# A block of gated delta rule and experts on one core: 8x8 diagonal blocks inverted on GpSimd, the order of the pieces laid out over four turns, and a pipelined first stage

## What is computed

```
q, k = l2norm(silu(conv4(h @ Wq))), l2norm(silu(conv4(h @ Wk)));  v = silu(conv4(h @ Wv))
g = -exp(A_log) * softplus(h @ Wa + dt_bias);  beta = sigmoid(h @ Wb)
for each token:  S = S * exp(g);  delta = (v - k S) * beta;  S = S + k^T delta;  o = (q * scale) S
o = rmsnorm(o, gnorm_w) * silu(h @ Wg);  out = h2 + (silu(ff @ W1) * (ff @ W3)) @ W2,  h2 = h + o @ Wo
```

## Time and profile before

| | |
|---|---|
| median of 3 runs | 2630.22 us (2629.96 to 2634.56) |
| profiled execution, its own time | 2633.98 us |
| its span | 2632.2 us |
| PE, PEld busy | 2466.6 (94%), 2063.6 us (78%) |
| DVE, ACT, POOL busy | 2057.6 (78%), 1689.0 (64%), 899.0 us (34%) |
| mean granted clock of TensorE | 0.967 |

### The profile page before, as it was taken

One profiled execution on the slowest core, in us unless ns is written; L12 is line 12 of the kernel. 1 busy time (PEld: TensorE's weight loads), 2 busy tenths in 40 slices (PEclk: granted clock), 3 DMA queues, 4 the chain that ended last, 5 costly groups with the idle time before them and its releaser, 6 DMA issues. The chain is left out here.

```text
span 2632.2 us, 59594 instructions
## 1 busy us (share of the span) xinstructions
PE 2466.6 (94%) x21984; PEld 2063.6 (78%) x21984; DVE 2057.6 (78%) x4303; ACT 1689.0 (64%) x3890; POOL 899.0 (34%) x1053
## 2 busy tenths in 40 slices
PE   1289999999999999999999999999999999789997
PEld 0168888888888888888888888888888888646655
DVE  3468888888888888888888888888888888535444
ACT  1157777777777777777777777777777777522221
POOL 0033444444444444444444444444444444100000
PEclk6589999999999999999999999999999999889998
DMA  2221121112111211121112111121112110031000
GB/s 98 86 57 40 41 60 42 41 41 60 42 41 42 60 41 41 42 60 41 42 41 56 45 42 41 52 49 42 41 45 56 41 42 14 1 121 32 33 6 11
DMA packets 148317, 120.45 MB, mean 46 GB/s; under 512 B 24305, under 2 KB 128698, under 8 KB 148034
## 3 DMA queue, kind: packets, MB, share of 16 engines
q1 hardware_dynamic: 148034, 116.66, 16.7%
HBM read 72.11 MB, written 2.54 MB: 28 GB/s over the span
## 5 line engine op out<-in xcount | busy, mean ns | idle before, releaser
L740 DVE TENSOR_TENSOR dr_w<-dr_ps,mask 128x512 bf16<-128x512 f32 x768 | 526.3, 685 | 90.5 <-PE dr_ps L556 89.7
L754 DVE SCALAR_TENSOR_TENSOR dr_y<-dr_ps,dr_cw,dr_y 128x255 f32<-128x255 f32 (+2 forms) x1152 | 475.8, 474 | 38.1 <-ACT dr_y L870 38.1
L856 ACT CAST dr_tn<-dr_ps 128x512 bf16<-128x512 f32 x640 | 375.0, 586 | 157.6 <-PE dr_ps L569 156.7
L859 ACT CAST dr_tt<-dr_ps 128x512 bf16<-128x512 f32 x768 | 459.2, 598 | 20.9 <-PE dr_ps L576 20.9
L653 PE MATMUL dr_ps<-dr_w,dr_am 128*128 128x96 f32 x3072 | 418.2, 279 | 9.5 <-ACT dr_w L916 2.1
L653 PEld LDWEIGHTS dr_ps<-dr_w,dr_am 128*128 128x128 f32 x3072 | 378.8, 193 | 32.3 <-ACT dr_w L916 24.5
L870 ACT ACTIVATE dr_y<-dr_ps,dr_cw 128x256 f32<-128x256 f32 x384 | 160.9, 470 | 222.2 <-PE dr_ps L593 222.1
L576 PE MATMUL dr_ps<-dr_tt,dr_w 128*128 128x128 bf16 x3072 | 297.6, 219 | 0.9 <-DVE dr_w L740 0.9
L556 PE MATMUL dr_ps<-dr_tn,dr_b 128*128 128x128 bf16 x3072 | 297.6, 219 | 0.0
L982 POOL TENSOR_SCALAR_AFFINE_SELECT dr_b<-dr_b 128x512 bf16<-128x512 bf16 x128 | 81.6, 637 | 506.9 <-ACT dr_b L906 506.9
L569 PEld LDWEIGHTS dr_ps<-dr_w,dr_tt 128*128 128x128 bf16 x2560 | 186.7, 101 | 84.5 <-issue 49.3
(11 more groups left out here) (188 smaller groups left out, 4784.2 us busy)
## 6 DMA issues: line engine op xcount, KB each, us to landing
dr_abc<-scr_a SPq DMA_DIRECT2D x64, 512.0 KB, 5.6
dr_qk<-dr_sy SPq DMA_DIRECT2D x384, 48.0 KB, 2.0
dr_hb<-hT SPq DMA_DIRECT2D x64, 256.0 KB, 2.5
dr_bcb<-scr_b SPq DMA_DIRECT2D x128, 64.0 KB, 4.7
dr_qk<-dr_sy SPq DMA_DIRECT2D x128, 32.0 KB, 1.9
ex_modb<-scr_mod SPq DMA_DIRECT2D x4, 1024.0 KB, 8.2
dr_wo<-in_Wo SPq DMA_DIRECT2D x1, 3072.0 KB, 10.9
dr_wv<-in_Wv SPq DMA_DIRECT2D x8, 384.0 KB, 4.0
```

Of the source, the lines that this page charges most:

```text
L740: v.tensor_tensor((tn if l == 0 else w16)[:, us, :], ps[:, (X0, X1)[g], :].rearrange("p (u n) -> p u n", u=QH), bc(mask[:, l, :], 1, QH), ...
L754: v.scalar_tensor_tensor(y[:, slot, x:T], ps[:, BANK[n], off:off + T - x], cw[:, t, TAPS - 1 - x:TAPS - x], y[:, slot, x:T], ALU.mult, ALU ...
L856: act.copy(tn[:, us, :], ps[:, (X2, X1)[g], :].rearrange("p (u n) -> p u n", u=QH)).then_inc(s["tn_ok"], 1)
L859: act.copy(dst, ps[:, (X0, X2)[g], :].rearrange("p (u n) -> p u n", u=QH)).then_inc(s["tt_ok"], 1)
```

## The change

**The inverse.** LEVELS goes from 7 to 4: the levels of sizes 1, 2 and 4 go, and the diagonal blocks of size BASE = 8 come from elsewhere. SP moves the diagonal 16x16 pieces of b16 to c16 (eight transfers for each iteration, piece `blocks`). PE spreads the rows of each block over its partitions with 14 products against a selection matrix (`rows`), ACT copies them to ab. POOL then solves all 8x8 blocks by substitution, in a copy and 14 instructions, each waiting for the one ahead (`base`). DVE widens the result to blocks of 32 in c32, transposes it, and writes tt and tn of 128x128 with two multiplies of 1024 elements (`expand`). Level 0 is now a full level with both products of merge2.

**The order.** PLAN is new: places up to 57.07, stage and slot as before (15 slots, depth 4, now over 64 + 3 turns too). values is later by a turn, base and expand stand at the end of the second turn, the merges in the third. The gate pieces come after decayed, in banks A0 and A1, and free them for proj of the next turn. hb is gone; PE reads hT itself. SP loads the gate weights apart from the others, after batch. The semaphores that counted passed waits are gone.

**The first stage.** All groups are written out and interleaved over the engines; the modulation's first 512 columns come first, are spread over the partitions by PE and not by way of DRAM; the remaining 1024 columns follow later. ACT centres, POOL takes half of the scaling, the step matmuls follow each group. Weights of the next stage (wqk, wv, cw, wo, gw) are loaded here.

```diff
-LEVELS = 7
+BASE = 8
+LEVELS = 4
+LVL0 = 3
...
+PLAN = ((0.41, ("proj", 0)), (1.58, ("taps", 0, 0)), (1.83, ("taps", 0, 1)), (1.87, ("proj", 1)),
+        (3.4, ("taps", 1, 0)), (4.13, ("silu", 0)), (5.57, ("taps", 1, 1)), (7.06, ("silu", 1)), (7.19, ("proj", 2)),
+        (8.17, ("taps", 2, 0)), (9.44, ("taps", 2, 1)), (9.53, ("gains",)), (10.1, ("norms",)), (10.15, ("keys",)),
+        (10.23, ("decays", 0)), (10.86, ("keys_scale",)), (11.0, ("decayed", 0, 0)), (11.07, ("decayed", 0, 1)),
+        (11.47, ("scores", 0)), (11.59, ("silu", 2)), (12.87, ("decays", 1)), (13.09, ("scores", 1)),
+        (13.39, ("decayed", 1, 0)), (13.6, ("decayed", 1, 1)), (13.76, ("negate", 0)), (13.94, ("gate", 0)),
+        (14.49, ("negate", 1)), (14.94, ("gate", 1)), (20.05, ("values", 0)), (21.7, ("values", 1)),
+        (25.51, ("rows",)), (27.18, ("base",)), (28.56, ("round", 0)), (29.84, ("expand",)),
+        (31.0, ("merge1", 0, 0)), (31.19, ("merge2", 0, 0)), (31.2, ("merge1", 0, 1)), (31.72, ("merge2", 0, 1)),
+        (31.77, ("merge1", 1, 0)), (32.28, ("merge2", 1, 0)), (32.77, ("merge1", 1, 1)), (34.03, ("merge2", 1, 1)),
+        (35.01, ("merge1", 2, 0)), (35.76, ("merge2", 2, 0)), (36.28, ("merge1", 2, 1)), (37.74, ("merge2", 2, 1)),
+        (38.13, ("merge1", 3, 0)), (38.59, ("merge2", 3, 0)), (38.74, ("merge1", 3, 1)), (38.82, ("merge2", 3, 1)),
+        (39.8, ("w0", 0)), (40.13, ("residual", 0, 0)), (40.72, ("delta", 0, 0)), (41.66, ("residual", 0, 1)),
+        (42.95, ("delta", 0, 1)), (43.63, ("state_out",)), (43.75, ("mean", 0)), (44.13, ("ks",)),
+        (45.27, ("w0", 1)), (45.87, ("gated", 0)), (46.18, ("residual", 1, 0)), (46.5, ("oT", 0)),
+        (46.7, ("delta", 1, 0)), (48.42, ("residual", 1, 1)), (50.02, ("wo", 0)), (50.69, ("delta", 1, 1)),
+        (52.48, ("acc", 0)), (53.27, ("out", 1)), (53.95, ("mean", 1)), (55.15, ("gated", 1)), (56.28, ("oT", 1)),
+        (56.8, ("wo", 1)), (57.07, ("acc", 1)))
...
+            def spread(b):
+                wait(pe, s["bc_free"], b - NBC + 1)
+                pe.matmul(ps[:, BC + b % NBC, :], bc(const[0:B, C_ID + b], 1, P), mod[:, 0:2 * D],
+                          start=True, stop=True).then_inc(s["bc_ps"], 1)
...
+            def blocks(it):
+                m = it % NB
+                sp.wait_ge(s["b16_ok"], (it + 1) * CH)
+                wait(sp, s["bc_ps"], it)
+                for n in range(P // (2 * BASE)):
+                    rows = slice(2 * BASE * n, 2 * BASE * (n + 1))
+                    sp.dma_start(c16[rows], b16[rows, m, :, rows]).then_inc(s["c_st"], 16)
...
+            def rows_(st):
+                it, m = st
+                pe.wait_ge(s["c_st"], (it + 1) * 16 * (P // (2 * BASE)))
+                wait(pe, s["tt_ok"], it * LEVELS * 2 - 1)
+                for j in range(BASE - 1):
+                    for h in range(2):
+                        last = pe.matmul(ps[:, X0, j * U * BASE:(j + 1) * U * BASE], sel[:, h, j, :],
+                                         c16[:, :, h * BASE:(h + 1) * BASE], start=(h == 0), stop=(h == 1))
+                last.then_inc(s["bc_ps"], 1)
...
-                pe.wait_ge(*((s["tap"], (it + 1) * NT * 3), (s["gs_ok"], it * CH + 1))[c])
+                if c == 0:
+                    pe.wait_ge(s["wg_ld"], (it // B + 1) * 16)
+                pe.wait_ge(s["am_ok"], it * 4 + 3 + c)
...
+            def expand(st):
+                it, m = st
+                v.wait_ge(s["xb_ok"], it + 1)
+                v.tensor_tensor(c32[:].rearrange("p u (r i) -> p u r i", r=4), bc(xb[:], 2, 4),
+                                bc(bc(const[:, C_QUART:C_QUART + 4], 1, U), 3, BASE), ALU.mult).then_inc(s["c32_ok"], 1)
+                v.wait_ge(s["c32_ok"], it + 1)
+                v.transpose(c32t[:].rearrange("p u i -> p (u i)"), c32[:].rearrange("p u i -> p (u i)")
+                            ).then_inc(s["c32t_ok"], 1)
+                wait(v, s["p3"], it * LEVELS * 2)
+                blk = bc(bd32[:].rearrange("p (n i) -> p n i", i=4 * BASE), 1, U)
+                v.tensor_tensor(tt[:].rearrange("p u (n i) -> p u n i", i=4 * BASE), bc(c32[:], 2, 4), blk,
+                                ALU.mult).then_inc(s["te_ok"], 1)
+                v.wait_ge(s["c32t_ok"], it + 1)
+                v.tensor_tensor(tn[:].rearrange("p u (n i) -> p u n i", i=4 * BASE), bc(c32t[:], 2, 4), blk,
+                                ALU.mult).then_inc(s["te_ok"], 1)
...
+            def base(st):
+                it, m = st
+                n = it * (2 * BASE - 2)
+                wait(pool, s["c32_ok"], it)
+                pool.tensor_copy(xb[:], bc(const[:, C_UNIT:C_UNIT + BASE], 1, U)).then_inc(s["xs"], 1)
+                pool.wait_ge(s["ab_ok"], it + 1)
+                for j in range(BASE - 1):
+                    left = BASE - 1 - j
+                    pool.wait_ge(s["xs"], n + 2 * j + 1)
+                    pool.tensor_tensor(xt[:, :, 0:left], bc(xb[:, :, j], 2, left), ab[:, j, :, j + 1:BASE],
+                                       ALU.mult).then_inc(s["xs"], 1)
+                    pool.wait_ge(s["xs"], n + 2 * j + 2)
+                    ins = pool.tensor_tensor(xb[:, :, j + 1:BASE], xb[:, :, j + 1:BASE], xt[:, :, 0:left], ALU.add)
+                    ins.then_inc(s["xb_ok"] if j == BASE - 2 else s["xs"], 1)
```

More of the change, by code:

```diff
@@ L58 @@
 ATANH = [1.0 / (2 * k + 1) for k in range(9)]
[L60 to L66, removed]
[7 rows of a table removed]
[L74 to L79, removed]
@@ L89, in wait @@
         eng.wait_ge(sem, value)
[L92 to L106, removed]
 class Chain:
@@ L242, in _, with steps @@
-            pe.wait_ge(beta_ok, 1)
+                        last = pe.transpose(ps[:, TR + k, j * P:(j + 1) * P], hn[:, g % 2, j, k * P:(k + 1) * P],
+                                            const[:, C_ID:C_ID + P])
+                    last.then_inc(s["tr_ps"], 1)
+            def steps(g):
+                pe.wait_ge(s["ht_ok"], (g + 1) * KT)
+                for w in range(2):
+                    for k in range(KT):
+                        last = pe.matmul(ps[H * g:H * (g + 1), (ZA, ZB)[w], :], wab[:, k, H * w:H * (w + 1)],
+                                         hT[:, k, g * GTOK:(g + 1) * GTOK], start=(k == 0), stop=(k == KT - 1))
+                    last.then_inc(s["z_ps"], 1)
@@ new lines, in _ @@
+            pe.wait_ge(s["c_ld"], 32)
+            pe.wait_ge(s["c_silu"], 1)
+            modulation(0, TMP).then_inc(s["mod_ps"], 1)
+            pe.wait_ge(s["id_ld"], 16)
+            pe.wait_ge(s["modr_ok"], 2)
+            for b in range(4):
+                spread(b)
+            pe.wait_ge(s["k_ld"], 16 * NK)
+            for g in range(GROUPS):
+                turn(g)
+                steps(g)
+                for b in (2 * g + 4, 2 * g + 5):
+                    if b < B:
+                        spread(b)
@@ L471, in delta_rule @@
         PIECES = ("merge1", "merge2", "w0", "delta", "residual", "ks", "out", "state_out", "mean", "gated", "oT", "wo",
-                  "acc", "proj", "silu", "taps", "gate", "norms", "gains", "decays", "keys", "keys_scale", "scores", "decayed", "negate",
+                  "acc", "rows", "base", "expand", "proj", "silu", "taps", "gate", "norms", "gains", "decays", "keys", "keys_scale", "scores", "decayed", "negate",
                   "values", "round")
@@ L721, in wo_ @@
                 last.then_inc(s["wo_ps"], 1)
-            on.update(merge1=merge1, merge2=merge2, proj=proj, norms=norms, gate=gate, keys=keys, scores=scores,
+            on.update(merge1=merge1, merge2=merge2, rows=rows_, proj=proj, norms=norms, gate=gate, keys=keys, scores=scores,
                       values=values, w0=w0, residual=residual, delta=delta, out=outputs, state_out=state_out, ks=ks,
@@ L837, in acc @@
                 v.tensor_tensor(at, at, ps[:, CO, 0:D], ALU.add).then_inc(s["acc_ok"], 1)
-            on.update(merge1=merge1, taps=taps, decays=decays, gains=gains, decayed=decayed, values=values,
+            on.update(merge1=merge1, expand=expand, taps=taps, decays=decays, gains=gains, decayed=decayed, values=values,
                       residual=residual, state_out=state, ks=ks, mean=mean, gated=gated, acc=acc)
```

543 lines of the change are left out of this document (308 added, 235 removed), and 7 rows, old and new, of the table PLAN.

## The result

The changed kernel takes 2653.81 us (median of 4 runs, 2652.96 to 2660.61), the kernel before 2632.31 us in the same comparison: ratio 1.0087, 95% interval 1.0067 to 1.0108. The profiled execution has a span of 2658.8 us against 2632.2, 26.6 us more.

A forecast was written before the change was run, and what follows sets the result against it. PE issue, almost without holes, was taken to bound the 33.2 us turn. From 2630 us, the first stage gave -55, the turns -7, start-up and drain +3: 2571 us, range 2465 to 2685.

The forecast's parts named there:

- head: All that comes before the first gains; the forecast had -55 us for the first stage and -4 for the start-up.
- tail: From the last gains to the end; the forecast had the last partial turn 7 us longer.
- PE saves three microseconds, and another ring closes the turn: Full turns: PE's sum falls from 33.2 to 30.0 us, but POOL and DVE work in line keeps the turn at 33.1.
- PE's own ring: PE's chain from norms to the next merge1 and back, with its waits for other engines, closing at 32.4 us.
- The walk round GpSimd's ring: Chain from expand's end over norms, gains, POOL's work, base and expand again, summed from row spacings to 33.0 us.
- The rival of the blocking: POOL and DVE block each other at expand, ring 1.0 to 1.2 us longer, turn 34.2, 2638 us; 13 in 100.
- The rival of the falling clock: PE's clock falls after waits in every turn, adding 2.8 us to its ring: turn 35.2, 2699 us; 14 in 100.
- The first stage: Work before the first projection, which comes at 73 us against 128.6: -55 us, between -45 and -65.
- after 90 us: Sign of a wrong forecast: a first projection later than this, where 68 to 78 us was the sign of right.
- PE up to 7 us per group: First stage: PE's time per group at half clock, beside DVE's 5.3 and ACT's 5.1; four groups end at about 40.
- The drain: End of the pipeline: the last batch ends 3.8 turns after its start, before 3.3, so +7 us.

The follow-up runs named there:

- base cut: The changed kernel with six of base's seven elimination steps left out, so the blocks aren't inverted: 2579.0 us (ratio 0.9786).
- the power late: The changed kernel with POOL's 2.6 us power (nrm) moved out of gains to a piece of its own ahead of the second gate: 2586.3 us (0.9817).
- power late and norms early: The changed kernel with POOL's power moved behind the gates and PE's norms products moved between the last merge1 and the last merge2: 2584.9 us (0.9809).
- the early scan: The changed kernel with DVE's second scan of a turn moved in front of decayed(0), over before base begins: 2602.0 us (0.9874).

## Why the prediction was wrong

The forecast said 2571, faster; the time is 2653.8, slower, inside the range of 2465 to 2685 in its upper part, on the side that had 22 in 100. Three terms of the sum were mis-sized, all in the same direction. Put in the parts used above (the forecast had 61 turns and the start-up beside them): head -59 forecast, -37.4 measured; turns 33.1 us, -0.05 each, forecast, +0.64 measured; tail +7 forecast, +23.7 measured. With 63 turns that is 21.6 + 63 x (33.79 - 33.1) + 16.7 = 81.8 us. The profiled spans differ by +26.6 where -59 was forecast, 85.6 us; the 3.8 left over are the forecast's -7 us for the turns, which it counted from 33.22 and not from the mean of 33.15. No single term turned the sign: by these parts the turns as measured would have left a gain of 12 us, with the head as measured it is a loss of 10, and with the tail the 26.6.

**PE saves three microseconds, and another ring closes the turn**: right, with the saving a little smaller. PE is busy 30.78 us in a turn at full clock, 2.3 less than the 33.1 before; the forecast had 30.0, 3.2 less. PE's own ring was put at 32.4; with base cut, where GpSimd's is out of the way, it is 32.6 with its share of half clock and 32.1 without.

**The walk round GpSimd's ring**: right in place, wrong in size. In the median turn, with the forecast in brackets: expand's end to the first operation of gains 17.85 us (17.7), from there to dg 0.86 (0.8), POOL from dg to base 7.37 (6.5), base 5.0 (5.5), the link to expand and expand 2.75 (2.2, and 0.3 for all links). Sum 33.8 in place of 33.0. So the step that failed is the price of POOL's stretch before base, which took the 0.91 us that the scan costs keys_scale, and of expand, whose last multiply took 0.67 more than 0.65. In the 17 turns in which the scan strikes base instead, the stretch is 6.6 and base 5.8. The rates taken were not at fault: undisturbed, base takes 5.0 us, less than forecast, and the multiply of 1024 elements 0.65 where 0.67 was taken. The two overruns, 1.6 us together, were partly made up by base: that the ring closed only 0.8 above its forecast is luck, and so is that the time stayed inside the range. The rival of the blocking was weighed at expand's first multiply only, where nothing happened, and with a price of 1.0 to 1.2 us. A ring walked with each engine's undisturbed durations misses the blocking; the second timeline has to be laid beside the first.

**The rival of the falling clock** came true as an event (0.50 for some 3 us, in 19 of 60 turns) and not as a cost: it lies on PE's ring, which had 1.1 us to spare. Once that ring binds, a turn with the fall takes 0.7 to 1.0 us more than one without (32.3 and 33.0 with the power late, 32.1 and 33.0 with base cut, 32.1 and 33.1 with power late and norms early), and about every second turn has it.

**The first stage**: the first projection came at 90.68 us against 73, and "after 90 us" had been named as the sign of being wrong. The first group was turned on PE at 24.8 us, where it had been expected through at about 12, and the last step matmuls of the four groups ended at about 66, not 40. Why the first group came 13 us late no run tested. Then the step "PE up to 7 us per group" was seen but put beside DVE's and ACT's work instead of between them. In two of four groups it stood ahead of the spread, so those groups took 14 us each (from PE's product at 26.42 to that at 40.74), where 12.7 had been measured before and 7 were forecast. The order of PE's queue accounts for the 8.4 us that turning it round gave back, of the 21.6 by which the head missed. From the groups' end to the projection it took 24 us where 33 were forecast, which hid 9 us of the miss.

**The drain**: the last batch's first merge comes 45.9 us after its gains (2232.8 to 2278.7); before, it came 17.0 us after (2229.9 to 2246.9). The order says why: from gains to the first merge it has 31.0 - 9.53 = 21.5 slots of 15 to a turn, before 14.39 - 5.68 = 8.7. That is 0.85 turns more between the last gains and the end, at 33.8 us a turn 29 us, and 28.9 were measured. From that merge to the experts' first product it takes 5.7 us less than before (57.1 against 62.8), with four levels instead of seven. The forecast compared the ends of the two plans, 3.8 and 3.3 turns, and so made the last partial turn 7 us longer; it should have counted turns from the moved piece to the end.

**What was right besides**: the transfers to c16 and the removed one to hb cost nothing that a wait of PE shows; PE waits once per turn for expand and DVE for base; base runs 5 to 6 us; POOL is busy 19.0 us a turn.

## What to carry to other kernels

When the bound engine loses work, walk every other ring that crosses the changed pieces with all the engines' timelines side by side, and price each pair of a DVE instruction with two inputs in SBUF and a POOL multiply at the same moment as if one waited for the other (the powers on POOL didn't block here). A blocked pair doesn't stay where one turn shows it: look at the durations of all turns before naming one instruction. Then look for the instruction in that ring which is not needed there: here one power of 2.6 us, moved into an idle stretch, was worth 67 us, three times what the change had cost. A deeper pipeline pays its depth again at the tail, in turns from the moved piece to the end, not in the difference of the plan's lengths. An order has to be retuned after each such step, because an edit that helped under one ring (the early scan, -0.81 us) cost 0.6 under the next. And a fall of the clock that some turns have and others don't is its own experiment: compare the turns of one run before building another.
